# Two edits in a two-layer graph-transformer kernel: a reordered first stage whose stores end under the attention, and output projections as three f32r passes with additions on GpSimd

## What is computed

```
# first stage
xn = layernorm(x)                                  # kept for later
y  = layernorm(xn) * ln1_g + ln1_b                 # input of the attention
# attention of either layer, q and k through exp feature maps
out = (q @ (k^T v)) / (q @ sum(k) + eps)           # [1250, 768]
# output projection, layer 0
h   = xn + out @ proj_w + proj_b
sum = x + h ;  y = layernorm(h) * ln2_g + ln2_b    # y feeds the MLP
# output projection, layer 1
sum = x + layernorm(xn + out @ W + b) * gamma + beta + gnn_bias
```

## Time and profile before

| | us |
|---|---|
| median of 3 runs (range) | 3432.07 (3430.57 to 3433.05) |
| the profiled execution: its time | 3428.94 |
| its span, first to last instruction | 3427.2 |
| TensorE, VectorE, ScalarE, GpSimd busy | 2888.5, 2312.9, 1449.7, 462.6 |
| mean granted TensorE clock | 0.933 |
| first stage | 3.4 to 85.3 |
| attention of layer 0 (perf0) | 85.3 to 561.8 |
| first projection (proj0) | 702.3 to 820.0 |
| second projection (proj1) | 2771.2 to 2882.8 |

### The profile page before, as it was taken

The page is one execution under the profiler, slowest core; times in us unless marked ns, Lnnn a source line. Parts: engine busy times, 40 slices in busy tenths (PEclk is TensorE's granted clock), DMA queues, the critical chain, the costliest instruction groups (busy, mean ns, idle before and its releaser), DMA issues. The chain is left out here.

```text
span 3427.2 us, 50208 instructions
## 1 busy us (share of the span) xinstructions
PE 2888.5 (84%) x17656; PEld 2481.1 (72%) x17656; DVE 2312.9 (67%) x4167; ACT 1449.7 (42%) x2424; POOL 462.6 (13%) x327
## 2 busy tenths in 40 slices
PE   1999996967999998887988599868999977887794
PEld 1999995745788998777986233248999955777794
DVE  4665652735851553998664888657788858998775
ACT  3464552213112332555243577521546512554345
POOL 2287885200000000000002310000000000000000
PEclk9999998988999999999999699979999988999997
DMA  8333325694211653623131311253311077212301
GB/s 249 85 49 57 47 33 134 213 220 98 77 44 56 184 174 98 170 66 80 35 75 29 98 40 45 55 167 120 72 46 45 23 178 212 76 50 78 84 21 47
DMA packets 255535, 319.45 MB, mean 93 GB/s; under 512 B 97933, under 2 KB 179342, under 8 KB 255208
## 3 DMA queue, kind: packets, MB, share of 16 engines
q1 hardware_dynamic: 177576, 272.11, 29.4%
q0 software_dynamic: 77760, 44.83, 6.6%
HBM read 236.35 MB, written 79.53 MB: 92 GB/s over the span
## 5 line engine op out<-in xcount | busy, mean ns | idle before, releaser
L195 POOL DMA_INDIRECT adj_d<-edge_val,edge_off x160 | 332.5, 2078 | 184.6 <-DVE edge_off L183 100.0
L3191 DVE TENSOR_TENSOR expert_wgel<-expert_gel,expert_wps 128x417 f32<-128x417 f32 (+1 forms) x384 | 203.0, 584 | 57.0 <-PE expert_wps L3116 46.6
L2102 PE MATMUL gat00att_ops<-gat00att_h,gat00att_p 125*125 x1600 | 198.2, 280 | 48.4 <-DVE gat00att_p L2076 48.4
L2102 PE MATMUL gat10att_ops<-gat10att_h,gat10att_p 125*125 x1600 | 195.9, 279 | 48.4 <-DVE gat10att_p L2076 48.4
L2102 PEld LDWEIGHTS gat00att_ops<-gat00att_h,gat00att_p 125*125 125x125 f32 x1600 | 183.8, 189 | 63.0 <-issue 63.0
L2102 PEld LDWEIGHTS gat10att_ops<-gat10att_h,gat10att_p 125*125 125x125 f32 x1600 | 184.1, 192 | 60.8 <-issue 60.8
L3163 ACT ACTIVATE expert_gel<-expert_hps 128x417 f32<-128x417 f32 (+1 forms) x384 | 193.5, 519 | 64.2 <-DVE expert_wgel L3191 52.5
L577 PE MATMUL perf_wide<-y_lo,perf_qk_hi 128*128 128x416 f32 (+1 forms) x432 | 154.9, 359 | 24.7 <-DVE perf_qk_lo L759 24.4
L1275 PE MATMUL fc_ps<-y_lo,fc_w_hi 128*128 128x512 f32 (+1 forms) x432 | 154.6, 358 | 22.3 <-DVE fc_w_lo L1317 22.3
L1428 PE MATMUL fc_ops<-fc_w_hi,fc_x_lo 128*125 128x384 f32 x480 | 163.7, 341 | 7.1 <-DVE fc_w_lo L1480 7.1
L715 ACT ACTIVATE perf_kphi<-perf_wide,perf_lnm 125x384 f32<-125x384 f32 (+1 forms) x180 | 95.7, 630 | 172.5 <-PE perf_wide L601 171.6
(11 more groups left out here) (491 smaller groups left out, 7932.0 us busy)
## 6 DMA issues: line engine op xcount, KB each, us to landing
fc_w<-in_L_mix_fc_w SPq DMA_DIRECT2D x96, 384.0 KB
adj_d<-edge_zero POOLq DMA_DIRECT2D x22, 546.9 KB
gat00proj_adj<-adj_d POOLq DMA_DIRECT2D x20, 546.9 KB, 7.0
perf_keys<-keys_d SPq DMA_DIRECT2D x20, 437.5 KB
gat00att_sh<-shift_d SPq DMA_DIRECT2D x16, 546.9 KB
sh<-shift_d SPq DMA_DIRECT2D x16, 546.9 KB
perf_w<-in_L_mix_qkv_w SPq DMA_DIRECT2D x18, 384.0 KB
perf_w<-in_L_mix_W_qkv SPq DMA_DIRECT2D x18, 384.0 KB
```

Of the source, the lines that this page charges most:

```text
L195: edges.nc.gpsimd.indirect_dma_start(out=edges.adj_flat[u].rearrange("(n a) -> n a", a=1), out_offset=bass.IndirectOffsetOnAxis(ap=edges.o ...
L2102: ins = pe.matmul(ops[0:TP, u, b, t * w:(t + 1) * w], p[:, s, (t0 + t) * TP:(t0 + t + 1) * TP], h[:, s, bass.ds(hd, 1), :], start=(s == 0 ...
L3191: dve.tensor_tensor(wgel[:, q % W, 0:cn], gel[:, q % 3, 0:cn], wps[:, q % 3, 0:cn], ALU.mult).then_inc(wgel_done, 1)
```

## The change

**First stage.** Statistics of pair g+2 are taken ahead, both low parts of pair g-1 come after the second normalising of g, and ACT's order follows. x now lives in a room that the attention uses later for its features (`LateRows`); SP no longer waits for the stores, and the attention's ACT does, before its first exponentials. The first two key blocks are loaded during the first stage (between the second and third store), and their counts stand at the attention's start; the other counts move two places ahead.

**Projections.** a^T and w are split into f32r high and low parts (ACT rounds, DVE subtracts), and the product takes three f32r passes of 12 matmuls, 36 a tile. a is loaded by tiles, w by blocks of 128 rows. Room is found by laying w under tiles 4 to 9 of x, whose loads wait for the split. GpSimd adds the bias to xn, in the second projection also the shift row to x (10 and 21 additions of 125 x 768, 31 in all).

```diff
+class LateRows:
+
+
+
+    def __init__(self, nc, name, sb):
+        self.room = sb(f"{name}_room", [128, NT * D])
+        self.x = self.room[0:TP, :].rearrange("p (t d) -> p t d", t=NT)
+        self.stored, self.stored_n = nc.alloc_semaphore(f"{name}_stored"), 32 * (NT // 2)
+
+
 class EdgeCounts:
 
...
@@ -249,8 +264,10 @@
                     tiles = slice(2 * g, 2 * g + 2)
                     sp.wait_ge(normed, 2 * g + 2)
                     move_rows(sp, tokens(normed_d)[:, tiles, :], x[:, tiles, :], stored)
-                sp.wait_ge(key_st, 32)
-                sp.wait_ge(stored, 32 * pairs)
+                    if g == 1:
+                        sp.wait_ge(key_st, 32)
+                        for u in range(edges.SLOTS):
+                            edges.load_keys(sp, u, u)
 
             @block.gpsimd
             def _(pool):
...
+                root(1)
                 for g in range(pairs):
-                    if g + 1 < pairs:
-                        root(g + 1)
+                    root2(g)
+                    if g > 0:
+                        keep(2 * g - 1)
+                    if g + 2 < pairs:
+                        root(g + 2)
                     keep(2 * g)
-                    if g + 1 < pairs:
-                        root2(g + 1)
-                    keep(2 * g + 1)
+                keep(NT - 1)
 
             @block.vector
             def _(dve):
...
                 for g in range(pairs):
-                    if g + 1 < pairs:
-                        take_stats(g + 1)
-                        low_part(2 * g)
-                        take_root(g + 1)
-                        low_part(2 * g + 1)
-                        second_norm(g + 1)
-                    else:
-                        low_part(2 * g)
-                        edge_weights()
-                        low_part(2 * g + 1)
+                    take_root(g)
+                    if g + 2 < pairs:
+                        take_stats(g + 2)
+                    second_norm(g)
+                    if g > 0:
+                        low_part(2 * g - 2)
+                        low_part(2 * g - 1)
+                low_part(NT - 2)
+                low_part(NT - 1)
 
 
...
@@ -428,8 +445,13 @@
         fx = 2 if per_head else 1
         wa, wb = S.sb("wa", [128, fx, m], F32R), S.sb("wb", [128, 2, m], F32R)
         v = S.sb("v", [TP, NT, 4, vw])
-        kphi = S.sb("kphi", [TP, NT, m])
-        qphi = S.sb("qphi", [128, mb_n, N])
+        if late is not None:
+            kphi = late.room[0:TP, 0:NT * m].rearrange("p (t m) -> p t m", t=NT)
+            qphi = late.room[:, NT * m:NT * m + mb_n * N].rearrange("p (b n) -> p b n", b=mb_n)
+            S.sems.append(late.stored)
...
+                if counted is not None:
+                    counted.load(sp, 2, 0)
+                    counted.load(sp, 3, 1)
                 with sp.Fori(0, HP // 2 - 1) as i:
                     sp.wait_ge(w_split, i * 3 + 3)
...
+                if late is not None:
+                    act.wait_ge(late.stored, late.stored_n)
                 with act.Fori(0, HP // 2 - 1) as i:
                     for u in range(2):
                         pair(i, u, False)
...
+                if counted is not None:
+                    counted.count(dve, 0, 0, 0)
+                    counted.count(dve, 1, 1, 0)
                 rests(0, (0,))
                 split_w(v_parts, 1)
                 rests(0, (1,))
...
+                def load_a(t):
+                    move_rows(sp, a[:, t, :], attn_d[t * TP:(t + 1) * TP, :], a_ld[t])
+
+                def load_w(kb):
+                    sp.dma_start(w[:, kb, :], w_d[kb * 128:(kb + 1) * 128, :]).then_inc(w_ld[kb], 16)
+
+                load_a(0)
+                for kb in range(KB):
+                    load_w(kb)
+                load_a(1)
                 move_rows(sp, bias[:], row_bcast(bias_d, TP), bias_ld)
                 load_tiles(h, xn_d, xn_ld, 0)
-                load_tiles(a, attn_d, a_ld, 1)
+                for t in range(2, 5):
+                    load_a(t)
                 for k, r in enumerate((gain, shift)):
                     if turn:
                         sp.dma_start(rows[:, k, :], r).then_inc(rows_ld, 16)
...
-                    if p == 2:
-                        load_tiles(a, attn_d, a_ld, 2)
-                    load_tiles(h, xn_d, xn_ld, p)
-                    load_tiles(x, x_d, x_ld, p)
+                load_tiles(h, xn_d, xn_ld, 1)
+                sp.wait_ge(w_split, KB)
+                load_tiles(x, x_d, x_ld, 1)
+                for t in range(5, NT):
+                    load_a(t)
+                load_tiles(h, xn_d, xn_ld, 2)
+                load_tiles(x, x_d, x_ld, 2)
                 if first is not None:
...
 
-                    pe.wait_ge(kept, nth["a", t] + 1)
+                    pe.wait_ge(kept, t + 1)
                     if t >= 2:
                         pe.wait_ge(h_read, t - 1)
-                    for c in range(2):
+                    for kb in range(KB):
                         if t == 0:
-                            pe.wait_ge(w_ld[c], 16)
-                        for kb in range(KB):
-                            ins = pe.matmul(hps[0:TP, t % 2, c * 512:c * 512 + 384], aT[:, t % 2, kb, :],
-                                            w[:, kb, c * 384:(c + 1) * 384], start=(kb == 0), stop=(kb == KB - 1))
+                            pe.wait_ge(w_split, kb + 1)
+                        for c in range(2):
+                            for n, (ap, wp) in enumerate(((aT_hi, w_lo), (aT_lo, w_hi), (aT_hi, w_hi))):
+                                ins = pe.matmul(hps[0:TP, t % 2, c * 512:c * 512 + half], ap[:, t % 2, kb, :],
+                                                wp[:, kb, c * half:(c + 1) * half], start=(kb == 0 and n == 0),
+                                                stop=(kb == KB - 1 and n == 2))
                     ins.then_inc(h_done, 1)
                     if turn and t >= 3:
                         turn_tile("y", t - 3)
...
                         act.wait_ge(h_done, t - 1)
-                    act.copy(aT[:, t % 2], tps[:, n % 2, 0:KB * 128].rearrange("p (kb n) -> p kb n", kb=KB)[:, :, 0:TP]
-                             ).then_inc(kept, 1)
+                    act.copy(aT_hi[:, t % 2], turned_a(t)).then_inc(a_high, 1)
+
+                def high_w(kb):
+                    act.wait_ge(w_ld[kb], 16)
+                    act.copy(w_hi[:, kb, :], w[:, kb, :]).then_inc(w_high, 1)
 
                 def keep_y(t):
...
+            @block.gpsimd
+            def _(pool):
+                def base(t):
+                    if t in first_of:
+                        pool.wait_ge(xn_ld[first_of[t]], 32)
+                    pool.tensor_tensor(h[:, t, :], h[:, t, :], bias[:], ALU.add).then_inc(based, 1)
+
+                def shift_row(t):
+                    if t in first_of:
+                        pool.wait_ge(x_ld[first_of[t]], 32)
+                    pool.tensor_tensor(x[:, t, :], x[:, t, :], rows[0:TP, 1, :], ALU.add).then_inc(shifted, 1)
+
+                pool.wait_ge(bias_ld, 32)
+                base(0)
+                base(1)
+                if not turn:
+                    pool.wait_ge(rows_ld, 96 if more is not None else 64)
+                    if more is not None:
+                        pool.tensor_tensor(rows[0:TP, 1, :], rows[0:TP, 1, :], more[:], ALU.add).then_inc(more_added, 1)
+                        pool.wait_ge(more_added, 1)
+                    shift_row(0)
+                    shift_row(1)
+                for t in range(2, NT):
+                    base(t)
+                    if not turn:
+                        shift_row(t)
+
             @block.vector
             def _(dve):
...
+                def low_a(t):
+                    dve.wait_ge(a_high, t + 1)
+                    dve.tensor_tensor(aT_lo[:, t % 2], turned_a(t), aT_hi[:, t % 2].bitcast(F32), ALU.subtract).then_inc(kept, 1)
+
+                def low_w(kb):
+                    dve.wait_ge(w_high, kb + 1)
+                    dve.tensor_tensor(w_lo[:, kb, :], w[:, kb, :], w_hi[:, kb, :].bitcast(F32),
+                                      ALU.subtract).then_inc(w_split, 1)
+
                 def project(t):
 
-                    if t in first_of:
-                        dve.wait_ge(xn_ld[first_of[t]], 32)
-                    steps_done.done(dve.tensor_tensor(h[:, t, :], h[:, t, :], bias[:], ALU.add))
+                    dve.wait_ge(based, t + 1)
                     dve.wait_ge(h_done, t + 1)
-                    steps_done.wait()
                     both = h[:, t, :].rearrange("p (c n) -> p c n", c=2)
                     got = hps[0:TP, t % 2, :].rearrange("p (c n) -> p c n", c=2)[:, :, 0:384]
                     dve.tensor_tensor(both, both, got, ALU.add).then_inc(h_read, 1)
...
                     if t == 0 and not turn:
                         dve.wait_ge(rows_ld, 96 if more is not None else 64)
```

(3 more changed lines are left out.)

114 lines of the change are left out of this document (62 added, 52 removed).

## The result

The changed kernel takes 3399.72 us, median of 4 runs (3394.48 to 3406.76), beside 3432.56 for the kernel before (4 runs, 3430.57 to 3436.07): ratio 0.9904, 95% interval 0.9891 to 0.9917. It is faster, by 33 us, where 60 were forecast, and lies above the range (3352 to 3393).

A forecast was written before the change was run, and what follows sets the result against it. TensorE was busy 84% of the span, but other things were taken to decide the changed stages. Terms -22.5 (start), -14.3, -10.6 and -12.2 gave -59.6, 3369.3; with 3.1 for the median, 3372 us, range 3352 to 3393.

The forecast's parts named there:

- Step 1: First stage's work: with statistics and roots taken ahead, the last low part ends at 55 instead of 75.2, -20 us.
- Step 2: End of first stage: without the stores' wait the attention starts 1 us after the last work instead of 10, -9.
- step 3: Attention's start: later bias columns and v's weights, small packets going one for one with zeros, give back 6.5 us.
- Step 4: Attention's end: GpSimd's additions end at 503, VectorE's last instruction decides, and the stage ends at 525, -14 us.
- the rival: The additions still end the attention, deciding from a start after 103 on; at 125 the total is 3393 us; chance 0.04.
- Step 5: First projection: f32r passes -9.4, start -3, GpSimd's additions holding VectorE +1.5; stated total -10.6 us.
- step 6: Second projection: tiles -9.6, start and stall -4.7, end -1.9, VectorE held +4; total -12.2 us.
- GpSimd holds VectorE: Projections: VectorE's additions and normalisings wait for whole GpSimd additions, 12.5 instead of 4 and 7 instead of 1.5: 3386; chance 0.20.
- Starved queue: Attention's start: bias columns behind SP's stores land only with the zeros' end, at 84, so 3387 us; chance 0.17.
- Three passes at the low clock: Projections: matmuls of all 20 tiles run at 1.2 GHz, 12.6 us a tile instead of 6.3, +126, 3498 us; chance 0.03.

The follow-up runs named there:

- all zeros late: Changed kernel, but GpSimd issues all 26 DMAs of zeros at the start of the attention's own list, none in the first stage: 3389.21 us, ratio 0.9841.
- projections alone: Kernel before with only the projections' part of the change: 3415.49 us, ratio 0.9927.
- by halves: Changed kernel, but only the first array is cleared in the first stage, from x's last pair on, the second at the attention's start: 3386.84 us, ratio 0.9862.

## Why the prediction failed

**Steps 1 and 2.** Step 1's work came as forecast (last low part at 55.2, 55 forecast), at an even better pace. Step 2 failed: "the attention then starts 1 us after the last work instead of 10", resting on "SP sits on its stores". I put VectorE's idle time down to the one wait in the program's text that I could see and that the change removed. The rows said otherwise: from 81 to 83 us only q0 is listed, GpSimd's queue, and SP's had been empty since 79. GpSimd's last zeros were issued by 42 us in both kernels, and I took it for done; its transfers were not. With these zeros moved behind the barrier, and nothing else changed, the attention starts at 56.1, as forecast. This is 28 us, of which step 3 would have given 4 back: 24 of the 34 that were missing. The projections are 7, other stages 2.4.

**Step 3.** Since the attention did not start early, it hardly ran: +2.4 instead of +6.5. Where it did run, with all zeros late, its mechanism was right (one packet for one) and its size too small, 11.0 us for v's weights instead of 4.5; with half of the zeros behind the barrier 3.3 to 5.1 in three runs. The bias columns cost nothing there.

**Step 4.** Right: GpSimd's additions left the end, and VectorE's last instruction decides, 14.2 (14.3). The additions themselves took 436 us instead of the 417 that the step carried over; that cost nothing, since they still end 15 us before VectorE. It rests on the counts standing at the attention's start, not on the earlier start. With an early start of the attention it can turn: in the run with all zeros late the additions begin at 106.7, past the 103 that the rival named, and decide again, 531.6 against VectorE's 524.7. The rival's mechanism is right, and it is what happened with all zeros behind the barrier; with half of them there VectorE's end decides again (526.5 against 523.9).

**Step 5.** Tiles: -10.0 without additions (51.9), forecast -9.4; start -2.7, forecast -3; holding 3.7 to 4.4, forecast 1.5; it was 1.9 in the run with the projections alone (53.7 us), and 6.6 and 7.0 in the runs with all zeros late and by halves (58.5 and 58.9 us). TensorE's wait was 1.9 in the profile of the result; the rest is the lower clock behind it, which the step has no term for. The sum was 1.7 too high in that profile and 1.4 too low in that of the projections alone, so this term moves from one run to the next by more than the miss. The step's own arithmetic is loose: seven times 1.4 is 9.8, not the 9.4 here or the 9.6 of step 6; 7.91/24 x 2 is 0.66, not 0.64; its printed terms add up to 10.9, not 10.6; and tiles of 7.7 and 7.0, which it names as signs, would be 8.0 and 10.6 us gained. TensorE was waited for 4.30 us in one tile of the first projection only, 2.2 to 3.7 in the others.

**Step 6.** Tiles -11.6 (48.0), forecast -9.6; start -2.4, forecast -4.7; end -1.5, forecast -1.9; holding and waits 8.8 to 10.2, forecast 4. The addition's own price was near, 1.83 us against 1.7 (1.69 by the estimate from GPSIMD Engine Reference, 3.1 Elementwise, of the Trainium skill), and it did stand in a row: ten such additions took 17.84 us in the kernel before. What was mis-sized is what the additions do to VectorE. The 4 is no sum of its own: it stands beside nine late additions and 1.1 us of slack a tile. In the profile, of seven tiles five had an instruction held, two of them two or three, and most holds take 1.4 to 1.5 us of a tile that had 1.1 to spare; TensorE waited 6.9 us for that, and lost 1.7 to the lower clock.

**The rivals.** "GpSimd holds VectorE", 0.20, is what happened in the projections; priced at 12.5 and 7 us for the two, measured at 8.8 and 3.7 in the profile of the result and at up to 10.6 and 7.0 in others. Against it stood that VectorE's two-input instructions are not longer beside GpSimd; that was said of the trace and is not so (2.92 instead of 0.69 us, above). The rule of SBUF — State Buffer, Who interferes with whom (the Trainium skill), agrees with these rows as far as they reach: two inputs in SBUF are held (0.96 to 2.48), one input in PSUM is not (0.94), a cast and a scaling are (0.54 to 2.18, 0.68 to 2.01). "Starved queue", 0.17, has its sign in the profile, VectorE idle until 84, but not its cause: SP's queue was empty from 65 on, and the stage itself had not begun. No case of mine had the start unmoved. The range left out the first two rivals together, whose sum, 3401, is near the 3400 measured; that is luck, as the start was held by something else. "Three passes at the low clock", 0.03, came in small: no tile starts cold by itself, but the sign that it named, a granted clock of 0.5 in the middle of the projections, is there behind TensorE's waits, for 3.4 us in each projection. Its row is misread: rows 11 are headed with a clock of 0.5, but the profile grants 1.00 there (84 to 92 us), although one matmul starts every 0.35 us.

## What to carry to other kernels

Before a wait is removed, ask of every engine what it still has outstanding at that moment, and read it from the queues: an idle engine whose DMAs are in flight can be the one that holds the barrier. Here long transfers issued by GpSimd were better off behind the barrier or started early enough. Count what large packets do to small ones that share the engines. A wait of TensorE can cost more than its length: look at the granted clock behind it. Before additions go to GpSimd, count how many of VectorE's instructions meet them with two SBUF inputs, and search the whole trace for such a pair, not only the stage that changes. Here VectorE did the same additions itself for less in the stages, in either projection, though the whole program's time does not resolve it.

## What was new about the hardware

A stage's end waited for transfers that GpSimd had issued, and the next stage began within some 4 us of their last packet (at 84.4, 72.4 and 63.0 us in three kernels), though no instruction of the program waited for them there; transfers issued by SP were not waited for (251 packets around a start at 57.05, 112 of them after it). Which part of the stage's end does this was not tried. GpSimd's addition of 125 x 768 takes 1.83 us undisturbed, and 1.47 when both inputs are the same tile. Beside it VectorE's instructions with two SBUF inputs took up to 2.48 us instead of 0.96, and GpSimd's own up to 2.6.
